# Channel attention on one core: VectorE's normalisation, its row statistics and the rounding of the next key in another order

## The chip, the cores and the metric

The kernel runs on one core of a Trainium2 chip. A core has TensorE (matmuls; PE in the profile), VectorE (DVE), ScalarE (ACT), GpSimd (POOL) and SyncE, which issues DMAs (SP). Each engine runs its own instructions in order, and semaphores join them. The metric is the device time of one execution in microseconds (us), as the median of several runs.

## The reference

Two layers of a gated cross-attention block on 16 x 64 rows of 512 elements. The change lies in the first of four sub-blocks, an attention over channels:

```
x = x + tanh(g_xattn[0]) * xattn0(layernorm(x), ctx)
x = x + tanh(g_ffn[0])   * clustered_linear(layernorm(x))
x = x + tanh(g_xattn[1]) * grouped_query_attention(layernorm(x), ctx, ctx, mask)
x = x + tanh(g_ffn[1])   * quantised_swiglu(layernorm(x))

def xattn0(x, init):                         # per batch: [64 channels, 512]
    q = einsum('dc,bct->btd', Wq, init) + bq
    k = einsum('dc,bct->bdt', Wk, init) + bk
    attention = softmax(einsum('btd,bds->bts', q, k), axis=-1)     # 512 x 512
    v = einsum('oc,bct->bto', Wv, x) + bv
    return einsum('bts,bsc->bct', attention, v)
```

Queries and keys are kept in two parts, a rounded one and its rest, so that a product in the short format keeps the precision of float32.

## The kernel before

`channel_attention` goes over eight tiles. A tile is 128 rows of x, that is two batches of 64 channels. Its scores are two times 512 x 512, cut into eight **units** of 128 x 512: units 0 to 3 belong to the first batch, 4 to 7 to the second. Every engine has its own function `tile(t, behind, ahead)` with a loop `for u in range(8)`, in which ifs on `u` put the other work of this tile, of the tile behind and of the tile ahead between the units' own steps. This order, written out by hand, is what each engine runs; nothing is sorted later.

One unit goes through the engines like this (lines of the profile):

- TensorE: `scores` (L423, L424), two matmuls into one of three banks `RR`. From unit 3 on they wait until the exponential three units back has freed the bank. The first unit of a batch (0 or 4) waits until VectorE has made `q_stk` and `k_lo` of that batch.
- VectorE: the negated row maximum `nmax` (L289), called "maximum u" below.
- ScalarE: the exponential with row sums (L192), `prob` and `zsum`.
- VectorE: `rz`, the reciprocal of the row sums (L267). GpSimd: `prob * rz` (L374), called "product u".
- TensorE: four transposes of `prob` (L431) into one of two banks `TP`, three units later. ScalarE (even units, L185) or VectorE (odd units, L271) copies the bank to `p_t`.

Between the units stand, for each tile:

- `project(t, n)` on TensorE (L400, L401): query (even n) and key (odd n) of batch n // 2, from `ctx_stk`. Those of the second batch of tile t stand in its unit 2, those of the first batch of tile t + 1 in unit 4.
- `qk_round` on ScalarE (L179): the rounded part, `q_stk` or `k_hi`, with its bias. `qk_rest` on VectorE (L255 for the query, L251 for the key): what the rounding left.
- `ctx_round` on ScalarE (L173) and `ctx_rest` on GpSimd (L357): the same for the context of the next tile, in unit 3.
- `normalize` on VectorE (L243): `xn` from x and the mean and deviation of its rows. TensorE's `values` (L409) reads it in unit 6.
- `outputs(t - 1)` on TensorE (L442): 16 matmul passes, in unit 3, right before the transposes of unit 0 and the scores of unit 4. `update(t - 1)` on VectorE (L277) adds them to x in unit 4, and `new_rows(t - 2)` (L283) takes the statistics of rows updated a tile before, for the next sub-block.

Constants that place the work: `OUTPUT = 3`, `PROJECT_A = 4`, `PROJECT_B = 2`, `UPDATE = 4`, `VALUE = 6`. Tiles 0, 1 and 7 are written out on VectorE, 2 to 6 are a hardware loop.

Of the kernel before, what the change touches and what calls it, by code (L numbers as in the profile page):

```python
# [66 lines left out]
def channel_attention(nc, d, c):  # L67
# [14 lines left out]
    with ExitStack() as ctx:  # L82
# [6 lines left out]
        def sem(name):  # L89
            return ctx.enter_context(nc.semaphore(name))  # L90
# [28 lines left out]
        s_sum, s_mv, s_var, s_rstd = sem("sums_ready"), sem("mean_var_ready"), sem("var_ready"), sem("rstd_ready")  # L119
# [11 lines left out]
        OUTPUT = 3  # L131


        PROJECT_A, PROJECT_B = 4, 2
# [26 lines left out]
        @block.scalar  # L161
        def _(act):
            act.dma_start(w_qk[:, :, :], d["WqkT"]).then_inc(s_wq, 16)
            act.dma_start(b_qk[:, :], d["b_qk"]).then_inc(s_wq, 16)
            act.dma_start(ident[:, :], d["ident"]).then_inc(s_par, 16)
            for b in range(2):
                act.dma_start(bv[:, b, :], d["bv"].partition_broadcast(P)).then_inc(s_par, 16)
            act.dma_start(tg[:, :], d["gates"].partition_broadcast(P)).then_inc(s_tg, 16)

            def ctx_round(t, b):  # L170

                act.wait_ge(s_ctx, 32 * t + 32)
                nc.scalar.activation(ctx_stk[:, b, :], ctx_two[:, b, :], ACT.Copy).then_inc(s_chi, 1)  # L173

            def qk_round(t, n):

                act.wait_ge(s_qk, 4 * t + n + 1)
                dst, is_k = (k_hi, 1) if n % 2 else (q_stk, 0)
                nc.scalar.activation(dst[:, n // 2, :], QK[n % 2][:, :], ACT.Identity,  # L179
                                     bias=b_qk[:, is_k:is_k + 1]).then_inc(qk_hi, 1)  # L180

            def evacuate(t, u):

                act.wait_ge(s_t, 8 * t + u + 1)
                nc.scalar.activation(p_t[:, u // 4, :, (u % 4) * P:(u % 4 + 1) * P],  # L185
                                     TP[0][:, :].rearrange("p (j t) -> p j t", j=KC),
                                     ACT.Copy).then_inc(pt_act, 1)

            def tile(t, behind, ahead):
                for u in range(8):  # L190
                    act.wait_ge(s_max, 8 * t + u + 1)
                    nc.scalar.activation(prob[:, u % 4, :], RR[u % 3][:, :], ACT.Exp,  # L192
                                         bias=nmax[:, u:u + 1], accum_out=zsum[:, u:u + 1])\
                      .then_inc(s_exp, 1)
                    if u == 1 and behind:
                        evacuate(t - 1, 6)
                    if u in (5, 7):
                        evacuate(t, u - 3)
                    if u == PROJECT_B + 1:
                        qk_round(t, 2)  # L200
                        qk_round(t, 3)
                    if u == OUTPUT and ahead:
                        ctx_round(t + 1, 0)
                        ctx_round(t + 1, 1)
                    if u == OUTPUT:
                        act.wait_ge(s_raw, 16)
                        nc.scalar.activation(ctx_hi[:, t, :], ctx_raw[:, t, :], ACT.Copy).then_inc(s_thi, 1)
                    if u == OUTPUT:
                        evacuate(t, 0)
                    if u == OUTPUT and not ahead:  # L210
                        act.wait_ge(s_w, 16)
                        nc.scalar.activation(w_hi[:, :, :], w_raw[:, :, :], ACT.Copy).then_inc(s_whi, 1)
                    if u == PROJECT_A and ahead:
                        qk_round(t + 1, 0)
                    if u == PROJECT_A + 1 and ahead:
                        qk_round(t + 1, 1)

            ctx_round(0, 0)
            act.wait_ge(s_wq, 32)
            nc.scalar.activation(w_qk_hi[:, :, :], w_qk[:, :, :], ACT.Copy).then_inc(s_wqk, 1)  # L220
            ctx_round(0, 1)
            qk_round(0, 0)
            qk_round(0, 1)
            act.dma_start(c["ctx_raw"][:, :, :], d["ctxT"].rearrange("(k p) n -> p k n", p=P)).then_inc(s_raw, 16)
            act.dma_start(w_raw[:, :, :], d["w_cl"].rearrange("(k p) n -> p k n", p=P)).then_inc(s_w, 16)
            act.dma_start(c["bias0"][:, :], d["bias0"].partition_broadcast(P)).then_inc(c["s_small"], 16)
            act.dma_start(c["assign_i"][:, :], d["assign"].partition_broadcast(CLUSTERS)).then_inc(c["s_small"], 16)
            act.dma_start(c["cluster_id"][:, :], d["cluster_ids"]).then_inc(c["s_small"], 16)
            act.wait_ge(s_tg, 16)
            nc.scalar.activation(tg[:, :], tg[:, :], ACT.Tanh).then_inc(s_tg, 1)  # L230
            tile(0, False, True)
            with act.Fori(1, TILES - 1) as t:
                tile(t, True, True)
            tile(TILES - 1, True, False)
            evacuate(TILES - 1, 6)

        @block.vector
        def _(dve):
# [3 lines left out]
            def normalize(t):  # L242
                nc.vector.tensor_scalar(xn[:, :], x_sb[:, t, :], mv[:, t, 0:1], rstd[:, t, :],  # L243
                                        ALU.subtract, ALU.mult).then_inc(s_xn, 1)
# [14 lines left out]
            def value(t):  # L259
                dve.wait_ge(s_v, t + 1)  # L260
                nc.vector.tensor_tensor(v_sb[:, :, :], OB[:, :].rearrange("p (j c) -> p j c", j=KC),
                                        bv[:, :, :].rearrange("p b c -> p (b c)").unsqueeze(1)
                                        .broadcast_to([P, KC, P]), ALU.add).then_inc(s_vsb, 1)

            def inverse(t, u):
                dve.wait_ge(s_exp, 8 * t + u + 1)
                nc.vector.reciprocal(rz[:, u:u + 1], zsum[:, u:u + 1]).then_inc(s_rz, 1)  # L267

            def evacuate(t, u):
                dve.wait_ge(s_t, 8 * t + u + 1)  # L270
                nc.vector.tensor_copy(p_t[:, u // 4, :, (u % 4) * P:(u % 4 + 1) * P],  # L271
                                      TP[1][:, :].rearrange("p (j t) -> p j t", j=KC))\
                  .then_inc(pt_dve, 1)

            def update(t):
                dve.wait_ge(s_o, t + 1)
                nc.vector.scalar_tensor_tensor(out=x_sb[:, t, :], in0=OB[:, :], scalar=tg[:, 0:1],  # L277
                                               in1=x_sb[:, t, :], op0=ALU.mult, op1=ALU.add)\
                  .then_inc(s_upd, 1)

            def new_rows(t):
                dve.wait_ge(s_upd, t + 1)
                nc.vector.bn_stats(c["bn6"][:, t, :], x_sb[:, t, :]).then_inc(s_sum, 1)  # L283

            def tile(t, behind, ahead):

                for u in range(8):
                    dve.wait_ge(s_r, 8 * t + u + 1)
                    nc.vector.tensor_reduce(nmax[:, u:u + 1], RR[u % 3][:, :], AX.X, ALU.max,  # L289
                                            negate=True).then_inc(s_max, 1)  # L290
                    if u == 0 and behind:
                        inverse(t - 1, 7)
                    if u and u != 4:
                        inverse(t, u - 1)
                    if u in (0, 2) and behind:
                        evacuate(t - 1, u + 5)
                    if u == PROJECT_B + 1:
                        qk_rest(t, 2)
                        qk_rest(t, 3)
                    if u == OUTPUT:  # L300
                        inverse(t, u)
                        if not behind:
                            dve.wait_ge(s_rstd, 1)
                        normalize(t)
                        if behind == 2:
                            new_rows(t - 2)
                    if u == UPDATE and behind:
                        update(t - 1)
                    if u in (4, 6):
                        evacuate(t, u - 3)  # L310
                    if u == PROJECT_A + 1 and ahead:
                        qk_rest(t + 1, 0)
                    if u == PROJECT_A + 2 and ahead:
                        qk_rest(t + 1, 1)
                    if u == VALUE + 1:
                        value(t)
# [16 lines left out]
            with dve.Fori(2, TILES - 1) as t:  # L333
                tile(t, 2, True)
# [1509 lines left out]
```

## Time and profile before

| | us |
|---|---|
| median of 3 runs | 847.76 |
| lowest and highest | 847.03, 848.78 |
| the profiled execution, its own time | 845.51 |
| its span, first to last instruction | 843.7 |
| channel attention within it | about 0 to 152 |
| VectorE busy over the whole span | 662.9 (79%) |
| TensorE busy over the whole span | 774.3 (92%) |

Channel attention takes the first 18% of the span. Times in the rows below are counted from the start of the span. A timeline row gives start, duration, engine, line, operation, tiles, shapes and, in square brackets, how long the engine sat idle before it and whose result ended that. Durations of one engine overlap a little: the next instruction starts before the last one's results are all written, so the cost of an instruction in a busy queue is the distance between starts, not the duration.

### The profile page before, as it was taken

What the parts mean: (1) busy time and instruction counts of PE and PEld (TensorE: products, weight loads), DVE (VectorE), ACT (ScalarE), POOL (GpSimd) and SP (SyncE); (2) the same over time, 40 slices, a digit from 0 to 9 for tenths busy, and PEclk for the clock granted to TensorE, in tenths of its full rate; (3) what the DMA queues carried; (4) which work ended last, traced back from release to release, by engine and by line L of the source; (5) the groups of instructions that cost most, each with busy time, mean ns of one, the idle gap of its engine ahead of it and who ended that gap; (6) DMA issues with size and microseconds to landing.
All of it is one profiled execution on the core that took longest, in us unless ns stands there. A gap on an engine that the chain in (4) does not pass through costs nothing.

```text
span 843.7 us, 12571 instructions
## 1 busy us (share of the span) xinstructions
PE 774.3 (92%) x4276; PEld 613.4 (73%) x4276; DVE 662.9 (79%) x1230; ACT 352.3 (42%) x1064; POOL 380.9 (45%) x324
## 2 busy tenths in 40 slices
PE   2898998888989999999999999999999999969975
PEld 1565565786867788888878888877888787757754
DVE  5788888888978877778788777787877778798972
ACT  2777776221334333333333333434333243237541
POOL 2787787415364433333253332434423333386541
PEclk9999999897999999999999999999999999989995
DMA  8310030101021111011020100102101020200101
GB/s 256 107 51 25 25 106 0 39 0 51 1 76 50 38 38 51 26 38 39 26 63 26 51 26 26 48 29 63 38 26 38 26 88 24 55 4 1 38 25 38
DMA packets 37460, 37.43 MB, mean 44 GB/s; under 512 B 2912, under 2 KB 27232, under 8 KB 37408
## 3 DMA queue, kind: packets, MB, share of 16 engines
q1 hardware_dynamic: 35184, 32.81, 13.3%
q10 hardware_dynamic: 2224, 3.94, 1.5%
q8 instruction: 31, 0.51, 0.3%
q14 instruction: 21, 0.17, 0.1%
HBM read 34.64 MB, written 2.10 MB: 44 GB/s over the span
## 4 chain that ended last, share of the span: by engine, by line
PE 63%; DVE 6%; POOL 4%; issue 3%; ACT 2%; POOLq 0%; DVEq 0%; ACTq 0%
PE QB L1478 6%; PE QB L1480 6%; PE SB L1598 6%; PE QB L1479 6%; PE ROW L1479 6%; PE ROW L1478 6%; PE ROW L1480 6%; PE KV L1478 4%; PE PB L1571 3%; PE KV L1479 3%; PE KV L1480 3%; DVE rope_b L1244 2%; PE KV L1662 2%; PE TB L1541 2%; POOL dense L976 1%
## 5 line engine op out<-in xcount | busy, mean ns | idle before, releaser
L976 POOL TENSOR_TENSOR dense<-rope_a,rope_b 128x512 f32<-128x512 f32 x62 | 79.4, 1280 | 167.5 <-DVE rope_b L1244 167.3
L1110 ACT ACTIVATE ot_hi<-PB 128x512 fp32r<-128x512 f32 x64 | 38.3, 599 | 198.4 <-PE PB L1571 198.2
L1101 ACT ACTIVATE e_sb<-masked,nmax 128x64 f32<-128x64 f32 x256 | 86.1, 337 | 58.1 <-DVE nmax L1273 57.7
L1478 PE MATMUL QB<-xT_hi,wq_lo 128*128 128x512 f32 x256 | 107.0, 418 | 0.0
L1479 PE MATMUL ROW<-wo_lo,ot_hi 128*128 128x512 f32 x256 | 101.7, 397 | 0.0
L1480 PE MATMUL QB<-xT_hi,wq_hi 128*128 128x512 f32 x256 | 101.7, 397 | 0.0
L1479 PE MATMUL QB<-xT_lo,wq_hi 128*128 128x512 f32 x256 | 101.5, 396 | 0.0
L1478 PE MATMUL ROW<-wo_hi,ot_lo 128*128 128x512 f32 x256 | 101.3, 396 | 0.0
L1480 PE MATMUL ROW<-wo_hi,ot_hi 128*128 128x512 f32 x256 | 101.0, 395 | 0.0
L1241 DVE TENSOR_TENSOR rope_a<-QB,rope 128x512 f32<-128x512 f32 x62 | 42.8, 691 | 72.7 <-PE QB L1480 72.5
L1282 DVE TENSOR_TENSOR p_sb<-e_sb,rz 128x256 f32<-128x256 f32 x64 | 86.8, 1356 | 2.2
L1244 DVE TENSOR_TENSOR rope_b<-QB,rope 64x512 f32<-64x512 f32 x124 | 85.4, 689 | 3.9
L374 POOL TENSOR_TENSOR prob<-prob,rz 128x512 f32<-128x512 f32 x64 | 66.3, 1045 | 22.7 <-DVE rz L267 21.6
L773 POOL TENSOR_TENSOR wq_lo<-raw,wq_hi 128x512 fp32r<-128x512 f32 x32 | 41.7, 1305 | 64.0 <-ACT wq_hi L765 64.0
L1598 PEld LDWEIGHTS SB<-k_rot,dense 128*128 128x128 f32 x512 | 64.3, 194 | 7.2 <-POOL dense L976 2.2
L1598 PE MATMUL SB<-k_rot,dense 128*128 128x64 f32 x512 | 67.0, 274 | 2.5 <-POOL dense L976 2.5
L192 ACT ACTIVATE prob<-RR,nmax 128x512 f32<-128x512 f32 x64 | 44.1, 690 | 34.6 <-DVE nmax L289 34.6
L1480 PEld LDWEIGHTS QB<-xT_hi,wq_hi 128*128 128x128 f32 x256 | 48.3, 189 | 11.7
L1480 PEld LDWEIGHTS ROW<-wo_hi,ot_hi 128*128 128x128 f32 x256 | 48.1, 188 | 11.7
L1478 PEld LDWEIGHTS ROW<-wo_hi,ot_lo 128*128 128x128 f32 x256 | 48.3, 188 | 11.5
L1479 PEld LDWEIGHTS ROW<-wo_lo,ot_hi 128*128 128x128 f32 x256 | 48.0, 188 | 11.0
L1479 PEld LDWEIGHTS QB<-xT_lo,wq_hi 128*128 128x128 f32 x256 | 48.7, 190 | 8.9
(200 smaller groups left out, 1902.2 us busy)
## 6 DMA issues: line engine op xcount, KB each, us to landing
raw<-in_wq SPq DMA_DIRECT2D x32, 256.0 KB, 2.7
raw<-in_wo SPq DMA_DIRECT2D x32, 256.0 KB, 2.6
ctx_two<-in_ctx SPq DMA_DIRECT2D x16, 256.0 KB, 3.8
x_sb<-in_x SPq DMA_DIRECT2D x8, 256.0 KB, 7.1
ctx_raw<-in_ctxT ACTq DMA_DIRECT2D x1, 2048.0 KB, 12.9
raw<-in_wv SPq DMA_DIRECT2D x8, 256.0 KB, 2.7
raw<-in_wk SPq DMA_DIRECT2D x8, 256.0 KB, 2.9
out<-x_sb SPq DMA_DIRECT2D x8, 256.0 KB, 2.0
```

The source lines that it names most:

```text
L192: nc.scalar.activation(prob[:, u % 4, :], RR[u % 3][:, :], ACT.Exp, bias=nmax[:, u:u + 1], accum_out=zsum[:, u:u + 1])\
L374: nc.gpsimd.tensor_tensor(prob[:, u % 4, :], prob[:, u % 4, :], rz[:, u:u + 1].broadcast_to([P, D]), ALU.mult).then_inc(s_p, 1)
L773: nc.gpsimd.tensor_tensor(lo, raw_piece(c, place, kind), hi, ALU.subtract).then_inc(c["s_piece"], 1)
L976: nc.gpsimd.tensor_tensor(dst, a, b, ALU.add).then_inc(s_rot, 1)
L1101: nc.scalar.activation(e_sb[:, r, :], masked[:, r, :], ACT.Exp, bias=nmax[:, r:r + 1], accum_out=zsum[:, r:r + 1]).then_inc(s_exp, 1)
L1241: nc.vector.tensor_tensor(a, v, cos.broadcast_to([P, 8, S]), ALU.mult).then_inc(s_parts, 1)
L1244: nc.vector.tensor_tensor(b[other], v[rows], sin[rows].broadcast_to([S, 8, S]), ALU.mult)\
L1282: nc.vector.tensor_tensor(p_sb[:, N % 2, :, :], e_sb[:, :, :], rz[:, :].unsqueeze(2).broadcast_to([P, 4, S]), ALU.mult).then_inc(s_p, 1)
L1478: nc.tensor.matmul(out, lhs[1], rhs[0], start=first, stop=False)
L1479: nc.tensor.matmul(out, lhs[0], rhs[1], start=False, stop=False)
L1480: return nc.tensor.matmul(out, lhs[0], rhs[0], start=False, stop=last)
L1598: mm = nc.tensor.matmul(SB_[:, S * a:S * a + S], q, keys[:, S * b:S * b + S], start=True, stop=True)
```

## The change

Three things are put elsewhere in the order of a tile; no instruction is added or removed, no size changes.

1. VectorE, unit 3: `normalize(t)` and the reciprocal of unit 3 stood behind `qk_rest(t, 2)` and `qk_rest(t, 3)`; now they stand ahead of them, and `normalize` also ahead of the reciprocal.
2. VectorE: `new_rows(t - 2)` stood at the end of unit 3; now it stands at the end of unit 2, ahead of maximum 3.
3. The first key of the next tile: ScalarE's `qk_round(t + 1, 1)` goes from unit 5 to unit 4, right behind the query's, and VectorE's `qk_rest(t + 1, 1)` from unit 6 to unit 5, again right behind the query's.

```diff
 (ScalarE, tile)
                     if u == PROJECT_A and ahead:
                         qk_round(t + 1, 0)
-                    if u == PROJECT_A + 1 and ahead:
                         qk_round(t + 1, 1)
 (VectorE, tile)
                     if u in (0, 2) and behind:
                         evacuate(t - 1, u + 5)
+                    if u == 2 and behind == 2:
+                        new_rows(t - 2)
+                    if u == OUTPUT:
+                        if not behind:
+                            dve.wait_ge(s_rstd, 1)
+                        normalize(t)
+                        inverse(t, u)
                     if u == PROJECT_B + 1:
                         qk_rest(t, 2)
                         qk_rest(t, 3)
-                    if u == OUTPUT:
-                        inverse(t, u)
-                        if not behind:
-                            dve.wait_ge(s_rstd, 1)
-                        normalize(t)
-                        if behind == 2:
-                            new_rows(t - 2)
 ...
                     if u == PROJECT_A + 1 and ahead:
                         qk_rest(t + 1, 0)
-                    if u == PROJECT_A + 2 and ahead:
                         qk_rest(t + 1, 1)
```

VectorE from the end of unit 2 to the start of unit 4, before, in the last tile (written out; the tiles of the loop have the same row of work): the first row is the copy that ends unit 2, the two maxima are 3 and 4.

```order
L271 COPY p_t<-TP 128x4x128
L289 TENSOR_REDUCE nmax<-RR 128x1
L267 RECIPROCAL rz<-zsum 128x1
L255 SCALAR_TENSOR_TENSOR q_stk<-QK,b_qk,q_stk 64x512
L251 SCALAR_TENSOR_TENSOR k_lo<-QK,b_qk,k_hi 128x512
L267 RECIPROCAL rz<-zsum 128x1
L243 TENSOR_SCALAR xn<-x_sb,mv,rstd 128x512
L283 BN_STATS bn<-x_sb 128x6
L289 TENSOR_REDUCE nmax<-RR 128x1
```

The same stretch now (line numbers are one or two lower):

```order
L270 COPY p_t<-TP 128x4x128
L282 BN_STATS bn<-x_sb 128x6
L288 TENSOR_REDUCE nmax<-RR 128x1
L266 RECIPROCAL rz<-zsum 128x1
L242 TENSOR_SCALAR xn<-x_sb,mv,rstd 128x512
L266 RECIPROCAL rz<-zsum 128x1
L254 SCALAR_TENSOR_TENSOR q_stk<-QK,b_qk,q_stk 64x512
L250 SCALAR_TENSOR_TENSOR k_lo<-QK,b_qk,k_hi 128x512
L288 TENSOR_REDUCE nmax<-RR 128x1
```

The statistics moved ahead of maximum 3, and the normalisation from behind the two rests to ahead of them, so that nothing stands between `k_lo` and maximum 4.

VectorE from maximum 5 to the copy of unit 6, before, in tile 0; the rests are those of tile 1's first batch:

```order
L289 TENSOR_REDUCE nmax<-RR 128x1
L267 RECIPROCAL rz<-zsum 128x1
L255 SCALAR_TENSOR_TENSOR q_stk<-QK,b_qk,q_stk 64x512
L289 TENSOR_REDUCE nmax<-RR 128x1
L267 RECIPROCAL rz<-zsum 128x1
L271 COPY p_t<-TP 128x4x128
L251 SCALAR_TENSOR_TENSOR k_lo<-QK,b_qk,k_hi 128x512
```

And now:

```order
L288 TENSOR_REDUCE nmax<-RR 128x1
L266 RECIPROCAL rz<-zsum 128x1
L254 SCALAR_TENSOR_TENSOR q_stk<-QK,b_qk,q_stk 64x512
L250 SCALAR_TENSOR_TENSOR k_lo<-QK,b_qk,k_hi 128x512
L288 TENSOR_REDUCE nmax<-RR 128x1
L266 RECIPROCAL rz<-zsum 128x1
L270 COPY p_t<-TP 128x4x128
```

The key's rest moved from behind maximum 6 and its copy to ahead of them. TensorE, GpSimd and SyncE run exactly the order they ran before.

## Rows read from the trace of the kernel before

**Rows 1.** Windows: stretch, length, busy us (x instructions) of each engine, PEclk, DMA.

```profile
core 0: us, PE busy (x) PEld busy (x) DVE busy (x) ACT busy (x) POOL busy (x), PEclk, DMA share, GB/s
69.12:85.21 16.09, 14.82 (x82) 9.29 (x84) 13.99 (x28) 11.89 (x27) 12.20 (x12) 1.00 0.12 33
155.00:160.00 5.00, 4.51 (x19) 4.51 (x20) 4.95 (x5) 2.50 (x5) 3.98 (x3) 0.50 0.18 53
300.00:500.00 200.00, 199.78 (x1119) 162.99 (x1118) 156.68 (x256) 72.77 (x262) 72.08 (x57) 1.00 0.13 36
```

**Rows 2.** Timeline of VectorE, maximum 0 to maximum 0 of tiles 3 and 4.

```profile
65.10 0.68 DVE L289 TENSOR_REDUCE nmax<-RR 128x1 f32<-128x512 f32 x1
...
69.12 0.69 DVE L289 TENSOR_REDUCE nmax<-RR 128x1 f32<-128x512 f32 x1 [0.48 <-PE RR L424]
...
71.24 0.76 DVE L255 SCALAR_TENSOR_TENSOR q_stk<-QK,b_qk,q_stk 64x512 fp32r<-64x512 f32 x1 [1.36 <-ACT q_stk L179]
72.03 0.75 DVE L251 SCALAR_TENSOR_TENSOR k_lo<-QK,b_qk,k_hi 128x512 fp32r<-128x512 f32 x1
...
72.76 1.18 DVE L243 TENSOR_SCALAR xn<-x_sb,mv,rstd 128x512 f32 x1
73.87 0.68 DVE L283 BATCH_NORM_STATS2 bn<-x_sb  x1
74.47 0.67 DVE L289 TENSOR_REDUCE nmax<-RR 128x1 f32<-128x512 f32 x1
...
76.32 0.67 DVE L289 TENSOR_REDUCE nmax<-RR 128x1 f32<-128x512 f32 x1
...
77.09 0.76 DVE L255 SCALAR_TENSOR_TENSOR q_stk<-QK,b_qk,q_stk 64x512 fp32r<-64x512 f32 x1
...
79.27 0.74 DVE L251 SCALAR_TENSOR_TENSOR k_lo<-QK,b_qk,k_hi 128x512 fp32r<-128x512 f32 x1
79.93 0.68 DVE L289 TENSOR_REDUCE nmax<-RR 128x1 f32<-128x512 f32 x1
...
81.19 0.68 DVE L289 TENSOR_REDUCE nmax<-RR 128x1 f32<-128x512 f32 x1
```

**Rows 3.** Timeline of TensorE: outputs, scores 4 and 5, scores 0 of the next tile.

```profile
69.01 3.65 PE L442 MATMUL OB<-p_t,v_sb 128*64 128x512 f32 x16
...
73.01 0.47 PE L423 MATMUL RR<-k_hi,q_stk 128*128 128x512 f32 x1
73.32 0.40 PE L424 MATMUL RR<-k_lo,q_stk 128*128 128x512 f32 x1
...
75.13 0.39 PE L424 MATMUL RR<-k_lo,q_stk 128*128 128x512 f32 x1
...
80.15 0.49 PE L423 MATMUL RR<-k_hi,q_stk 128*128 128x512 f32 x1 [0.91 <-DVE k_lo L251]
```

**Rows 4.** Timeline of GpSimd: products 7 and 2, then the context's rests.

```profile
65.94 1.04 POOL L374 TENSOR_TENSOR prob<-prob,rz 128x512 f32<-128x512 f32 x1 [0.22 <-DVE rz L267]
...
69.96 1.04 POOL L374 TENSOR_TENSOR prob<-prob,rz 128x512 f32<-128x512 f32 x1 [0.72 <-DVE rz L267]
72.38 2.72 POOL L357 TENSOR_TENSOR ctx_stk<-ctx_two,ctx_stk 64x512 fp32r<-64x512 f32 x2 [1.38 <-ACT ctx_stk L173]
```

**Rows 5.** Timeline of ScalarE: exponential 4 and the read of its sums.

```profile
75.17 0.69 ACT L192 ACTIVATE prob<-RR,nmax 128x512 f32<-128x512 f32 x1 [1.29 <-DVE nmax L289]
75.76 0.19 ACT L192 ACTIVATION_READ_ACCUMULATOR prob<-RR,nmax 128x1 f32 x1
```

**Rows 6.** Timeline of VectorE: maximum 5 of tile 0, maximum 0 of tiles 1 and 7.

```profile
28.65 0.69 DVE L289 TENSOR_REDUCE nmax<-RR 128x1 f32<-128x512 f32 x1 [0.28 <-PE RR L424]
...
33.53 0.68 DVE L289 TENSOR_REDUCE nmax<-RR 128x1 f32<-128x512 f32 x1
...
129.47 0.68 DVE L289 TENSOR_REDUCE nmax<-RR 128x1 f32<-128x512 f32 x1
```

**Rows 7.** Timelines of VectorE and GpSimd: normalisation and product 3 of tile 7.

```profile
137.12 0.53 DVE L243 TENSOR_SCALAR xn<-x_sb,mv,rstd 128x512 f32<-128x512 f32 x1
...
137.28 1.26 POOL L374 TENSOR_TENSOR prob<-prob,rz 128x512 f32<-128x512 f32 x1 [1.93 <-DVE rz L267]
```

## Prediction

> **What bounds the kernel now.** I looked first at where the change can act: only in channel attention, about 0 to 152 us. The windows [rows 1] show one tile of its loop, 16.09 us: VectorE is busy 13.99 us of it, TensorE 14.82 us, ScalarE and GpSimd about 12 us each. Two engines are nearly full and neither is quite, so the chain through both decides. The granted clock is 1.00 there (2.4 GHz).
>
> The timeline of VectorE [rows 2] gives the period from one maximum 0 to the next: 65.10 to 81.19, 16.09 us. I cut it at maximum 4 (74.47) into 9.37 and 6.72 us. In the first part VectorE is idle twice: 0.48 us ahead of maximum 3, for the scores, and 1.36 us ahead of the query's rest, for ScalarE's rounding. In the second it is never idle for long. TensorE [rows 3] waits 0.91 us ahead of scores 0 of the next tile, for the key's rest. So now the chain is: VectorE from maximum 0 on, through product 7 on GpSimd [rows 4] and the scores of unit 3 on TensorE back to maximum 3; then ScalarE's rounding, the two rests, the normalisation, the statistics, maximum 4; then VectorE's own queue to maximum 0.
>
> **Normalisation, unit 3.** Behind `k_lo` it costs 73.87 - 72.76 = 1.11 us between starts, all on the chain [rows 2]. Now it stands in the 1.36 us in which VectorE waits for ScalarE. It is 0.53 us long in tile 7 and 1.18 us in the loop [rows 7, 2], where it starts 0.38 us after GpSimd began the context's rests [rows 4]. In its new place it comes right behind a reciprocal whose product GpSimd is about to start. That is the situation of tile 7: the normalisation starts at 137.12 and takes 0.53 us, and the product, starting at 137.28, takes 1.26 instead of 1.04 us [rows 7, 4]. I take 0.53 us. Even 1.18 us would fit: from about 69.8 to 71.0, and the query's rest starts at 71.24. GpSimd loses some 0.2 us, but it has 1.38 us of idle time behind product 2 [rows 4]. Cost 0, gain 1.11 us of VectorE's chain. If the cover were gone it would cost 0.44 to 1.1 us.
>
> The 0.53 and the 1.18 us are to me one instruction with and without GpSimd on the shared way to memory. The Trainium skill (SBUF — State Buffer, Who interferes with whom) says that VectorE's two-port instructions and GpSimd's lock each other out, and that the one to issue first holds the ports for its whole length. By that rule the moved normalisation wins if it starts first, as in tile 7; if product 2 won, the normalisation would be held behind it, and that is rival A.
>
> **Statistics, unit 2.** They cost 74.47 - 73.87 = 0.60 us on the chain [rows 2]. Ahead of maximum 3 lies an idle time of 0.48 us, so they push it by at most 0.12 us, and by some 0.05 us if counted from where the copy lets the next instruction start. What hangs on maximum 3 is exponential 3, both roundings and both rests, and then scores 4. The key's rest ends at 72.03 + 0.75 = 72.78, and TensorE comes to scores 4 at 73.01 only, since the 16 output passes started at 69.01 [rows 3]. There are 0.23 us of room, so the push is covered. Bounds: 0, and 0.60 us if nothing covers it, of which 0.60 - 0.2 = 0.4 us would reach scores 4. I take 0, being nearest to the idle time in the row.
>
> **What is late next at maximum 4.** With 1.71 us gone from VectorE ahead of it, maximum 4 no longer waits for VectorE but for TensorE. The second matmul of scores 4 starts at 73.32 and lasts 0.40 us; with 0.04 us to the reader that is 73.76 instead of 74.47 [rows 3, 2]. The matmuls before it do not get earlier: they follow scores 3, which come from product 7, which starts at 65.94, right after maximum 0. So maximum 0 to maximum 4 becomes 73.76 - 65.10 = 8.66 us instead of 9.37. Only 0.71 of the 1.71 us are gained; the rest turns into a wait for TensorE.
>
> **The pair in unit 5.** The same instructions run between maximum 4 and the next maximum 0, in another order. Adding distances between starts [rows 2]: maximum 4 to 5, 1.85; on to the query's rest 0.77; on to the key's 0.79; on to maximum 6, 0.66; maximum 6 to 7 and 7 to 0 have the same three kinds of work each (a maximum, a reciprocal, a copy or sum), 1.26 each. Sum 6.59 us. The present order takes 6.72 us, the other bound. I take 6.6, since each of its distances was measured in that neighbourhood. Could anything be late inside it? Scores 5 are ready at 75.13 + 0.39 + 0.04 = 75.56 and maximum 5 now wants to start at 73.76 + 1.85 = 75.61: just in time. The key's rounding now runs ahead of exponential 5. Exponential 4 runs 0.70 us behind its maximum and takes 0.78 us with its sums [rows 5], the two roundings about 0.6 us each, so the key is rounded by about 76.4, well before VectorE wants it at 75.61 + 0.77 + 0.79 = 77.2. Maximum 6 comes at 77.8, exponential 6 ends 1.5 us later at 79.3, and scores 0 of the next tile can then start, instead of at 80.15 [rows 3], where they waited for the key's rest. They need about 0.8 us until they can be read, 80.1; maximum 0 comes at 73.76 + 6.6 = 80.4. So the wait of 0.91 us on TensorE goes, and VectorE's queue decides here.
>
> **The sum.** New period 8.66 + 6.6 = 15.26 us against 16.09. From maximum 0 of tile 1 (33.53) to that of tile 7 (129.47) lie six periods, 95.94 us [rows 6] (tile 1 has no statistics and is shorter). Now 6 x 15.26 = 91.56: a gain of 4.4 us. In tile 0, maximum 5 waits for TensorE and stays at 28.65; from there to 33.53 are 4.88 us, now 0.77 + 0.79 + 0.66 + 1.26 + 1.26 = 4.74: 0.1 us. Tile 7 rounds no next context and its maximum 4 follows TensorE's output passes almost at once already; nothing there but the shift. Together 4.5 us. Channel attention ends in a barrier of all engines, and the later parts run no changed instruction, so the gain should arrive at the end whole: the profiled execution would be 845.51 - 4.5 = 841.0. That execution lies 2.25 us under the median, so the median becomes 847.76 - 4.5 = 843.3 us.
>
> **Rivals.**
> A. *A smaller gain.* GpSimd gets the ports first: the normalisation ends at 69.96 + 1.04 + 0.53 = 71.53, the query's rest comes 0.3 us late, the key's ends near 73.1 to 73.2 and scores 4 slip by up to 0.2 us; six times that leaves 3.3 us. With 6.72 for the second part 0.7 us more go: 2.6 us, 845.2. For it: the 1.18 us in the loop. Against it: tile 7. Chance 0.18, taking 844.4 to 846.
> B. *No gain.* The waits move on: the statistics are uncovered (0.6 us late at maximum 3) and the normalisation is blocked as well. Then the query's rest starts 0.9 us late and scores 4 0.75 us late, and the period is 8.66 + 0.75 + 6.72 = 16.1, as now: 847.8. It needs both bad ends in every tile; the idle times in the rows speak against it. It is also what one would see if an order of semaphores I did not see held maximum 4. Chance 0.13.
> C. *Slower.* The parts behind start at another moment, and TensorE's clock there falls for longer. At 155 to 160 us, behind the idle time at the barrier, the granted clock is 0.50, that is 1.2 GHz, while TensorE is busy 4.51 of 5 us [rows 1]. At that level TensorE's work takes double the time, so each further us spent there costs half a us. The gain of 4.5 us is eaten when 9 us more run at 1.2 GHz, and at 13 us more the kernel is slower by 2 us: 849.8. Against it: from 300 to 500 us TensorE is busy 199.78 of 200 us at 1.00 [rows 1], and the idle time at the barrier does not change. Chance 0.07.
>
> **How the numbers follow.** The forecast has 0.62. About 0.2% (1.7 us) is what a measurement of this kernel can tell from no change. Forecast and A are faster, 0.80; B is the same, 0.13; C is slower, 0.07. The range: below, the forecast less another 1.4 us (medians of three runs spread over 1.75 us, and the second part might be a little shorter still), 841.9; above, A and the edge of B, where all bounds but one are bad (a gain of 1 us), 846.7. That leaves out most of B and C.
>
> **What the changed profile would show.** Right: maxima 0 of the loop 15.2 to 15.4 us apart; the normalisation at 0.53 us between maximum 3 and the query's rest, the product beside it 1.26 us; maximum 4 with an idle time of 0.7 to 1 us ahead of it, released by TensorE's scores; the wait of scores 0 for the key's rest gone; everything behind the barrier shifted by 4 to 5 us. Wrong: the normalisation at over 1.4 us, a query's rest more than 2.4 us behind maximum 3, scores 4 waiting for `k_lo`, or exponential 5 waiting for the key's projection. The whole would be wrong if the period fell and the end did not come earlier; then the clock windows behind 153 us are the place to look.

## The result and the profile after

| | before | after |
|---|---|---|
| median, us | 847.03 (7 runs) | 841.98 (7 runs) |
| lowest and highest, us | 845.32, 848.78 | 840.2, 843.5 |
| ratio, 95% interval | | 0.9941, 0.9927 to 0.9955 |
| the profiled execution, us | 845.51 | 842.73 |
| its span, us | 843.7 | 840.9 |

The change made the kernel 5.0 us faster; the interval of the ratio is 3.8 to 6.2 us. The forecast was a gain of 4.5 us and a time of 843.3 us, in a range from 841.9 to 846.7 us. The measured 841.98 us lie just above the lower end of that range. Of the 1.3 us below the forecast, 0.7 us come from the kernel before, whose median is 847.76 us over three runs and 847.03 over seven, and some 0.5 us from the gain.

The windows of the changed kernel, with one tile of the loop and a piece of tile 0 (columns as in [rows 1]):

```profile
core 0: us, PE busy (x) PEld busy (x) DVE busy (x) ACT busy (x) POOL busy (x), PEclk, DMA share, GB/s
67.11:82.38 15.27, 14.69 (x82) 9.33 (x80) 13.34 (x30) 11.88 (x28) 12.23 (x12) 1.00 0.11 34
...
28.00:31.00 3.00, 3.00 (x10) 2.41 (x9) 1.38 (x2) 1.99 (x5) 2.84 (x4) 0.50 0.00 0
```

A tile of the loop takes 15.27 us, 16.09 before. VectorE's busy time in it fell from 13.99 to 13.34 us although it runs the same instructions: that is the normalisation, 1.18 us before and 0.53 now. The second line, with a granted clock of 0.50, is a surprise and has a section of its own below.

VectorE, from maximum 0 of a tile to its maximum 7; it answers to [rows 2]:

```profile
67.11 0.68 DVE L288 TENSOR_REDUCE nmax<-RR 128x1 f32<-128x512 f32 x1
...
69.97 0.67 DVE L270 COPY p_t<-TP 128x512 f32<-128x512 f32 x1
70.56 0.68 DVE L282 BATCH_NORM_STATS2 bn<-x_sb  x1
71.16 0.67 DVE L288 TENSOR_REDUCE nmax<-RR 128x1 f32<-128x512 f32 x1
71.75 0.15 DVE L266 RECIPROCAL rz<-zsum 128x1 f32<-128x1 f32 x1
71.82 0.53 DVE L242 TENSOR_SCALAR xn<-x_sb,mv,rstd 128x512 f32 x1
72.68 0.16 DVE L266 RECIPROCAL rz<-zsum 128x1 f32<-128x1 f32 x1 [0.33 <-ACT prob L192]
73.26 0.76 DVE L254 SCALAR_TENSOR_TENSOR q_stk<-QK,b_qk,q_stk 64x512 fp32r<-64x512 f32 x1 [0.41 <-ACT q_stk L179]
74.05 0.75 DVE L250 SCALAR_TENSOR_TENSOR k_lo<-QK,b_qk,k_hi 128x512 fp32r<-128x512 f32 x1
75.76 0.69 DVE L288 TENSOR_REDUCE nmax<-RR 128x1 f32<-128x512 f32 x1 [0.96 <-PE RR L422]
...
77.62 0.68 DVE L288 TENSOR_REDUCE nmax<-RR 128x1 f32<-128x512 f32 x1
...
78.41 0.76 DVE L254 SCALAR_TENSOR_TENSOR q_stk<-QK,b_qk,q_stk 64x512 fp32r<-64x512 f32 x1
79.20 0.75 DVE L250 SCALAR_TENSOR_TENSOR k_lo<-QK,b_qk,k_hi 128x512 fp32r<-128x512 f32 x1
79.86 0.68 DVE L288 TENSOR_REDUCE nmax<-RR 128x1 f32<-128x512 f32 x1
...
81.12 0.68 DVE L288 TENSOR_REDUCE nmax<-RR 128x1 f32<-128x512 f32 x1
```

The single wait of 1.36 us ahead of the query's rest is now the normalisation and two waits of 0.33 and 0.41 us. The new wait is the 0.96 us ahead of maximum 4, and TensorE's scores (L422) end it. TensorE, output passes and scores 4, as in [rows 3]; the first row is scores 0 of the tile:

```profile
66.14 0.50 PE L421 MATMUL RR<-k_hi,q_stk 128*128 128x512 f32 x1 [0.32 <-ACT prob L192]
...
71.01 3.65 PE L440 MATMUL OB<-p_t,v_sb 128*64 128x512 f32 x16
...
75.01 0.47 PE L421 MATMUL RR<-k_hi,q_stk 128*128 128x512 f32 x1
75.32 0.40 PE L422 MATMUL RR<-k_lo,q_stk 128*128 128x512 f32 x1
```

Scores 4 run right behind the output passes and their transposes. The key's rest ended at 74.05 + 0.75 = 74.80, 0.21 us before they started. Scores 0 no longer wait for a key's rest (0.91 us before) but 0.32 us for exponential 6. GpSimd, product 2 and the context's rests, as in [rows 4]:

```profile
71.98 1.26 POOL L372 TENSOR_TENSOR prob<-prob,rz 128x512 f32<-128x512 f32 x1 [0.75 <-DVE rz L266]
74.40 2.53 POOL L355 TENSOR_TENSOR ctx_stk<-ctx_two,ctx_stk 64x512 fp32r<-64x512 f32 x2 [1.15 <-ACT ctx_stk L173]
```

Product 2 is 0.22 us longer, the context's rests are 0.19 us shorter than before (2.72). The normalisation used to start 0.38 us behind the start of the context's rests and now starts 0.16 us ahead of product 2: the collision moved from the one to the other.

### The profile page after: what moved, and what is told of

It is laid out like the page before. It is cut to its first block, busy times and chain, and to the rows that moved or that the text cites. A ratio compares the mean times of both kernels' runs of the same rounds, so it can differ in the third digit from the quotient of the medians.

```text
span 840.9 us, 12571 instructions
## 1 busy us (share of the span) xinstructions
PE 772.4 (92%) x4276; PEld 612.2 (73%) x4276; DVE 658.5 (78%) x1230; ACT 352.2 (42%) x1064; POOL 381.1 (45%) x324
## 4 chain that ended last, share of the span: by engine, by line
PE 61%; DVE 7%; POOL 4%; issue 3%; ACT 2%; POOLq 0%; DVEq 0%
PE SB L1596 6%; PE QB L1476 6%; PE QB L1478 6%; PE QB L1477 6%; PE ROW L1477 6%; PE ROW L1476 6%; PE ROW L1478 6%; PE KV L1476 4%; PE PB L1569 3%; PE KV L1478 3%; PE KV L1477 3%; DVE rope_b L1242 2%; PE KV L1660 2%; PE TB L1539 2%; POOL dense L974 1%
## 5 line engine op out<-in xcount | busy, mean ns | idle before, releaser
L771 POOL TENSOR_TENSOR wo_lo<-raw,wo_hi 128x512 fp32r<-128x512 f32 x32 | 41.2, 1297 | 30.7 <-ACT wo_hi L763 30.7
```

Of the source, the lines that this page charges most:

```text
L771: nc.gpsimd.tensor_tensor(lo, raw_piece(c, place, kind), hi, ALU.subtract).then_inc(c["s_piece"], 1)
```

## The experiments

All kernels stand beside the kernel before on the same chip. Two measures are given. The first is the ratio of the times, with its interval, turned into us of 847. The second comes from the profile of each: the period of the loop, its parts from maximum 0 to 4 and from 4 to the next 0, and six tiles, from maximum 0 of tile 1 to maximum 0 of tile 7, against 95.94 us [rows 6]. The last two columns, tile 0 (maximum 0 of tile 0 to that of tile 1) and the output passes of the last tile, are read in the section on the clock.

| kernel | time against before, us | period | 0 to 4 | 4 to 0 | six tiles | tile 0 | last passes |
|---|---|---|---|---|---|---|---|
| before | | 16.09 | 9.38 | 6.72 | 95.94 | 14.39 | 3.65 |
| before, second profile | +0.8 (-0.6 to +2.1) | 16.08 | 9.36 | 6.72 | -0.1 | 16.64 | 5.35 |
| after | -5.0 (-6.2 to -3.8) | 15.27 | 8.65 | 6.62 | -4.3 | 16.83 | 3.65 |
| after, second profile | -5.1 (-6.9 to -3.4) | 15.27 | 8.65 | 6.62 | -4.3 | 16.83 | 5.35 |
| norm_only | -2.4 (-3.6 to -1.3) | 15.40 | 8.65 | 6.74 | -3.6 | 17.43 | 3.65 |
| stats_only | -2.0 (-3.3 to -0.8) | 15.51 | 8.78 | 6.73 | -2.9 | 16.66 | 3.65 |
| pair_only | -0.8 (-2.2 to +0.4) | 15.96 | 9.37 | 6.59 | -0.8 | 16.61 | 3.65 |
| undo_stats | -4.7 (-6.1 to -3.2) | 15.27 | 8.65 | 6.62 | -4.3 | 16.55 | 3.65 |
| norm_unit2 | +0.3 (-0.6 to +1.4) | 16.08 | 9.46 | 6.62 | -0.1 | 16.79 | 5.35 |
| early_project | -2.9 (-4.1 to -1.7) | 15.70 | 9.08 | 6.62 | -1.7 | 16.27 | 3.65 |
| pe_filled | -5.9 (-7.3 to -4.7) | 15.27 | 8.66 | 6.62 | -4.3 | 14.11 | 3.65 |
| pe_filled_both | -5.3 (-7.0 to -3.4) | 15.28 | 8.66 | 6.62 | -4.3 | 13.38 | 3.65 |
| rests_mid | -5.4 (-6.9 to -3.8) | 15.27 | 8.65 | 6.61 | -4.3 | 14.43 | 3.65 |
| rests_filled | -6.1 (-7.5 to -4.7) | 15.27 | 8.65 | 6.62 | -4.3 | 14.20 | 3.65 |

**One part alone: normalisation.** My theory was that TensorE takes over at maximum 4 as soon as the normalisation is gone from behind the key's rest, with the statistics still there. The rival was that the parts add up.

```diff
                     if u == OUTPUT:
+                        if not behind:
+                            dve.wait_ge(s_rstd, 1)
+                        normalize(t)
                         inverse(t, u)
-                        if not behind:
-                            dve.wait_ge(s_rstd, 1)
-                        normalize(t)
-                        if behind == 2:
-                            new_rows(t - 2)
+                    if u == PROJECT_B + 1:
+                        qk_rest(t, 2)
+                        qk_rest(t, 3)
+                    if u == OUTPUT and behind == 2:
+                        new_rows(t - 2)
```

> Only the normalisation (with the reciprocal of unit 3) stands ahead of the two rests; statistics stay at the end of unit 3, behind the key's rest, and the next key is rounded and its rest made where they were. Theory (the cover decides, and TensorE takes over at maximum 4): the normalisation at 0.53 us; the key's rest ends near 72.8, the statistics take 0.60 us up to 73.3 (times of the tile shown for before), still ahead of 73.76, when TensorE has the scores; so maximum 4 waits about 0.4 us for scores and maximum 0 to maximum 4 is 8.66 us as in the changed kernel. Maximum 4 to maximum 0 stays 6.72 us. Period of the loop 15.38 to 15.40 us, change against before -3.7 to -4.3 us. Rival (the three parts add up, statistics give 0.60 us of their own): period 16.08 - 1.11 = 14.97 us at best or 15.87 us if only the 0.2 us that the statistics leave are gained.

VectorE in norm_only, from the key's rest to maximum 4:

```profile
74.06 0.75 DVE L251 SCALAR_TENSOR_TENSOR k_lo<-QK,b_qk,k_hi 128x512 fp32r<-128x512 f32 x1
74.73 0.68 DVE L283 BATCH_NORM_STATS2 bn<-x_sb  x1
75.79 0.69 DVE L289 TENSOR_REDUCE nmax<-RR 128x1 f32<-128x512 f32 x1 [0.38 <-PE RR L424]
```

The period is 15.40 us and 0 to 4 is 8.65, as expected; the statistics sit in the wait and 0.38 us of it are left. The time fell less than the six tiles did, 2.4 against 3.6 us, and misses the -3.7 that was expected at least. Its one profile has the longest tile 0 of all, 17.43 us; whether that is why stays open.

**One part alone: statistics.**

```diff
+                    if u == 2 and behind == 2:
+                        new_rows(t - 2)
...
-                        if behind == 2:
-                            new_rows(t - 2)
```

> Only the statistics are moved, from the end of unit 3 to the end of unit 2. Theory: maximum 3 comes up to 0.05 us later, the normalisation stays behind the key's rest at 1.18 us, and maximum 4 comes 0.55 us earlier than before, right behind the normalisation and with no wait for TensorE. Period of the loop 16.08 - 0.55 = 15.53 us, in the five tiles 2 to 6 only: change against before -2.7 us. Rival (statistics in unit 2 push maximum 3 by their 0.60 us and all behind it): period 16.1 us, no change.

VectorE in stats_only, the end of unit 3:

```profile
74.31 1.19 DVE L243 TENSOR_SCALAR xn<-x_sb,mv,rstd 128x512 f32 x1
75.42 0.68 DVE L289 TENSOR_REDUCE nmax<-RR 128x1 f32<-128x512 f32 x1
```

Maximum 4 follows the normalisation with no wait, the period is 15.51 us (15.53 expected), and maximum 0 to 3 is 4.05 us instead of 4.02: the push by the statistics is 0.03 to 0.04 us. Alone, this part gives 0.58 us a tile.

**One part alone: the key pair.**

```diff
                         qk_round(t + 1, 0)
-                    if u == PROJECT_A + 1 and ahead:
                         qk_round(t + 1, 1)
...
                         qk_rest(t + 1, 0)
-                    if u == PROJECT_A + 2 and ahead:
                         qk_rest(t + 1, 1)
```

> Only the next key is moved: rounded in unit 4, its rest made in unit 5. Theory: VectorE's queue from maximum 4 to maximum 0 goes from 6.72 to 6.60 us because maximum 6 and its reciprocal no longer stand behind the query's rest, nothing else moves, maximum 4 stays with VectorE. TensorE's wait of 0.91 us ahead of scores 0 goes down but gives nothing. Period 15.96 us, change against before -0.8 us. Rival (the wait of 0.91 us on TensorE was part of the chain): period 15.2 to 15.4 us, -4 us or more.

4 to 0 fell from 6.72 to 6.59 us and 0 to 4 stayed: period 15.96, as expected. TensorE in pair_only, scores 0:

```profile
81.22 0.50 PE L421 MATMUL RR<-k_hi,q_stk 128*128 128x512 f32 x1 [0.85 <-ACT prob L192]
```

TensorE's wait of 0.91 us for the key's rest went, and a wait of 0.85 us for exponential 6 took its place; VectorE's queue sets maximum 0 as before, so the wait for the key's rest was not part of the chain. The time alone could not tell this from no change.

**One part undone: statistics.** The changed kernel with `new_rows(t - 2)` back behind the key's rest.

> The changed kernel with the statistics put back to the end of unit 3, behind the key's rest (normalisation and key pair stay moved). Theory: the statistics fit into the 0.96 us that VectorE waits for scores 4 in the changed kernel, so the wait there shrinks to about 0.4 us and the period stays 15.27 us; change against before as the changed kernel, -4.5 to -5 us. Rival (the statistics' move gives a gain of its own): period 15.3 + 0.6 = 15.9 us, -1.5 to -2 us against before.

The wait ahead of maximum 4 shrinks from 0.96 to 0.38 us and the period stays 15.27 us. VectorE in undo_stats:

```profile
73.68 0.68 DVE L282 BATCH_NORM_STATS2 bn<-x_sb  x1
74.74 0.69 DVE L288 TENSOR_REDUCE nmax<-RR 128x1 f32<-128x512 f32 x1 [0.38 <-PE RR L422]
```

So in the changed kernel the move of the statistics is worth nothing. A move that gives 2.9 us in six tiles alone gives none beside the normalisation's, which gives 3.6 alone and leaves 0.4 us of room behind it: both remove work ahead of the same maximum, and TensorE caps the sum at 0.7 us a tile.

**The normalisation over a running product.** It is put ahead of the statistics in unit 2, where GpSimd is in product 1.

```diff
+                    if u == 2:
+                        if not behind:
+                            dve.wait_ge(s_rstd, 1)
+                        normalize(t)
                     if u == 2 and behind == 2:
                         new_rows(t - 2)
                     if u == OUTPUT:
-                        if not behind:
-                            dve.wait_ge(s_rstd, 1)
-                        normalize(t)
                         inverse(t, u)
```

> The changed kernel with the normalisation in unit 2, between the copy that ends the unit and the statistics, so that it starts about 70.6 us in the tile shown, while GpSimd is in the middle of product 1 (70.2 to 71.2). Theory (whichever of the two starts first keeps the other out): the normalisation is held until product 1 ends and takes about 1.1 us instead of 0.53; maximum 3 comes 1.1 us later, through the roundings scores 4 comes 0.9 us later, period of the loop 16.2 us, against before 0 to +1 us. Rival (no such lock, 0.53 us anywhere): maximum 3 comes 0.45 us later, scores 4 0.3 us later, period 15.55 us, against before -3 us.

VectorE in norm_unit2:

```profile
71.13 0.96 DVE L242 TENSOR_SCALAR xn<-x_sb,mv,rstd 128x512 f32 x1
72.01 0.68 DVE L282 BATCH_NORM_STATS2 bn<-x_sb  x1
```

GpSimd in the same kernel, products 0 and 1:

```profile
69.77 2.04 POOL L373 TENSOR_TENSOR prob<-prob,rz 128x512 f32<-128x512 f32 x2 [0.21 <-DVE rz L266]
```

The same instruction takes 0.96 us when it starts 0.68 us before the product's end, and 0.53 when it starts ahead of one. It is held, or slowed, by 0.43 us, a little less than until the product's end by its row. Placed here the normalisation costs 0.88 us between starts, and no wait of VectorE covers it; all of the change's gain is gone: period 16.08. Of these 0.88 us the rival gave 0.45 to the place alone. My 16.2 was 0.12 too high, for the most part because I had counted 1.1 us instead of 0.88.

**Projections earlier.** If TensorE's row of work from product 7 to scores 4 caps the gain, taking the projections of the second batch out of it should help.

```diff
-        PROJECT_A, PROJECT_B = 4, 2
+        PROJECT_A, PROJECT_B = 4, 1
...
                         normalize(t)
+                        qk_rest(t, 2)
+                        qk_rest(t, 3)
                         inverse(t, u)
-                    if u == PROJECT_B + 1:
-                        qk_rest(t, 2)
-                        qk_rest(t, 3)
```

> The changed kernel with the second batch's query and key projected in unit 1 instead of 2, rounded on ScalarE in unit 2, ahead of exponential 3; VectorE makes their rests in unit 3 as before, now between the normalisation and the reciprocal of unit 3. Theory (maximum 4 waits for TensorE's row of work from product 7 on: transposes, projections, scores 3, output passes, scores 4): without the projections in that row the output passes start as soon as VectorE's last copy of the tile behind is there, about 0.25 to 0.3 us earlier, maximum 0 to maximum 4 becomes 8.35 to 8.4 us, the period 14.95 to 15.0 us, and the time falls by 1.5 to 2 us below the changed kernel's. Rival (it is the key's rest that holds scores 4): it is ready earlier now as well, by 0.8 us, so the period would fall by up to 0.8 us, to 14.5 us. Third case (the output passes themselves or GpSimd hold): period unchanged at 15.27 us.

None of the three cases came: the period rose to 15.70 us. VectorE in early_project, maximum 0, maximum 2, the copy of the tile behind and maximum 4:

```profile
67.86 0.68 DVE L288 TENSOR_REDUCE nmax<-RR 128x1 f32<-128x512 f32 x1
...
70.75 0.69 DVE L288 TENSOR_REDUCE nmax<-RR 128x1 f32<-128x512 f32 x1 [0.89 <-PE RR L421]
...
71.43 0.67 DVE L270 COPY p_t<-TP 128x512 f32<-128x512 f32 x1
...
76.96 0.69 DVE L288 TENSOR_REDUCE nmax<-RR 128x1 f32<-128x512 f32 x1 [1.51 <-PE RR L421]
```

TensorE in the same kernel, scores 2 and the output passes:

```profile
70.33 0.39 PE L421 MATMUL RR<-k_lo,q_stk 128*128 128x512 f32 x1
...
72.21 3.65 PE L439 MATMUL OB<-p_t,v_sb 128*64 128x512 f32 x16 [0.59 <-issue]
```

The projections now stand ahead of scores 2, and maximum 2 waits 0.89 us. VectorE's copy of the tile behind starts 71.43 - 67.86 = 3.57 us after maximum 0 instead of 69.97 - 67.11 = 2.86 us. The output passes need that copy: they stand 0.59 us idle and start 0.11 us behind its end, 72.21 - 67.86 = 4.35 us after maximum 0 against 71.01 - 67.11 = 3.90 us in the changed kernel. That is about what the period lost, 0.43 us. I had counted what stood ahead of scores 3 and had not looked at what waits for scores 2.

## TensorE's clock in tile 0 and at the end

The span fell by 2.8 us only, while six tiles give 4.3. Maximum 0 of tile 1 is at 36.58 us, 3.05 us later than before: 0.61 us of that stand ahead of maximum 0 of tile 0 (19.75 against 19.14 us), 2.44 us in tile 0. For tile 0 the window 28 to 31 us above shows why: the granted clock is 0.50 there, 1.2 GHz. TensorE in the changed kernel, scores 4 of tile 0:

```profile
28.02 0.63 PE L422 MATMUL RR<-k_lo,q_stk 128*128 128x512 f32 x1
```

The same matmul before, where the window 24 to 28 us has 1.00:

```profile
26.39 0.39 PE L424 MATMUL RR<-k_lo,q_stk 128*128 128x512 f32 x1
```

So 3.05 us were lost up to tile 1 and 4.34 gained in six tiles: 1.3 us earlier at maximum 0 of tile 7. The last output passes of channel attention keep that distance. Before they are:

```profile
146.78 3.65 PE L442 MATMUL OB<-p_t,v_sb 128*64 128x512 f32 x16 [0.83 <-issue]
```

And in the changed kernel:

```profile
145.50 3.65 PE L440 MATMUL OB<-p_t,v_sb 128*64 128x512 f32 x16 [0.83 <-issue]
```

From their end to the end of the span are 693.3 us before and 691.8 after. These are the other 1.5 us of the 2.8, in a part of the kernel where no instruction was changed. In the fourteen profiles of the table this part takes 691.0 to 694.5 us; what moves it was not followed further.

At the start of the trace the matmuls tell the clock and the window does not. The window 20 to 24 us of the changed kernel reads 1.00, while its matmuls last 0.63 us:

```profile
20.00:24.00 4.00, 4.00 (x12) 3.03 (x11) 2.14 (x6) 2.31 (x6) 2.04 (x2) 1.00 1.03 398
```

```profile
20.69 0.63 PE L422 MATMUL RR<-k_lo,q_stk 128*128 128x512 f32 x1
```

Is it the change? The kernel before was profiled again, and so was the changed one.

> The kernel before, unchanged, for a second profile. Theory (whether TensorE's clock rises during the first scores is settled anew in every execution, whatever the kernel): the loop's periods are 16.08 us again, and tile 0 (maximum 0 to maximum 0) is either 14.4 us, as in the first profile, or 16.5 to 17.4 us, as in the changed kernel and four of the experiments; the span differs from 843.7 us by about the same 2 to 3 us in the second case. Rival (the long tile 0 belongs to the changed order): tile 0 is 14.4 us again.

> The changed kernel, unchanged, beside the two below on the same chip. Loop periods 15.27 us; against before -4.5 to -5.1 us; tile 0 at 14.3 or at 16.5 to 17.4 us.

The kernel before, second profile, windows in tile 0 and over the last output passes, and these passes:

```profile
core 0: us, PE busy (x) PEld busy (x) DVE busy (x) ACT busy (x) POOL busy (x), PEclk, DMA share, GB/s
...
28.00:30.00 2.00, 2.00 (x7) 1.67 (x8) 1.69 (x3) 1.00 (x3) 2.00 (x2) 0.50 0.00 0
...
149.80:155.10 5.30, 5.30 (x16) 1.70 (x16) 3.39 (x9) 0.00 (x0) 4.93 (x2) 0.68 0.01 3
```

```profile
149.77 5.35 PE L442 MATMUL OB<-p_t,v_sb 128*64 128x512 f32 x16 [0.83 <-issue]
```

Its tile 0 takes 16.64 us, its span 847.0, 3.3 us more than in the first profile of the same kernel. So the long tile 0 does not need the changed order; the first profile of before happened to be without it. The short one came with the changed order too, in rests_mid below, which fills nothing (14.43 us). Whether the change alters how often either comes is not shown. A second place of that kind are the last output passes: 5.35 us, with a granted clock of 0.68, instead of 3.65 in three of the fourteen profiles of the table, one of the kernel before and one of the changed kernel among them. Comparing before's second profile with the first of after, both with a long tile 0, maximum 0 of tile 1 stands at 36.58 us in both, and that of tile 7 at 132.45 and 128.18: 4.3 us from the six tiles, and the remaining 1.8 of 6.1 us in the span are the last passes (1.7 us) and what lies behind.

**Filling TensorE's idle time.** Transposes of a constant, whose results nobody reads: 18 in tile 0 ahead of scores 4, and in the second kernel 36 more ahead of the first scores.

```diff
+                    if u == OUTPUT and not behind:
+                        for _ in range(18):
+                            nc.tensor.transpose(OB[:, 0:P], w_v[:, :], ident[:, :])
```

> The changed kernel with 18 more transposes on TensorE in tile 0 only, behind the transposes of unit 0 and ahead of scores 4, into the bank OB that nobody reads before it is written anew. They add no result; they fill the idle time of about 3 us in which TensorE waits for the key's rest. Theory (the 3 us by which tile 0 was longer in the changed kernel's trace are TensorE's clock: matmuls of 0.63 us instead of 0.39 us up to 31 us): with TensorE busy there the clock is at 2.4 GHz from about 26 us on at the latest, maximum 0 of tile 0 to that of tile 1 falls from 16.8 us to 14.5 to 15 us, and the median is 1.5 to 2.5 us below the changed kernel's. Rival (the longer tile 0 comes from the moved work): tile 0 stays at 16.6 us or longer and the median is the changed kernel's or up to 1 us above.

> As the run before it, with 36 more such transposes ahead of tile 0, in the 8 us in which TensorE waits for the first key's rest. Theory (clock): the first scores run at 2.4 GHz too, maximum 0 to maximum 3 of tile 0 falls from about 4.1 to about 3.2 us, tile 0 takes 14.3 us or less and the median is 2 to 4 us below the changed kernel's. Rival (the clock does not depend on that idle time): as the changed kernel, or later where the transposes are still running when the key's rest is ready.

TensorE in pe_filled_both:

```profile
14.64 5.74 PE L471 MATMUL OB<-ident,w_v 128*128 128x128 f32 x36 [4.21 <-DMA w_v<-in_WvT]
...
20.46 0.39 PE L422 MATMUL RR<-k_lo,q_stk 128*128 128x512 f32 x1
```

With TensorE busy beforehand the first scores run at 0.39 us; in all other profiles they take 0.63. Maximum 0 to 3 of tile 0 falls to 2.33 us (3.0 to 4.2 elsewhere) and tile 0 to 13.38. That part of the theory is shown, by one profile against thirteen. But the filling work had to wait for the transfer of `w_v` until 14.64 and ran until 20.4 us, so maximum 0 came 1.2 us late, and the time gained nothing over the changed kernel. In the one profile of pe_filled the matmuls ran at 0.40 us from 20.9 us on, ahead of the filling at 22.6, so it shows nothing on the filling in tile 0; its times (839.5 to 843.4 us in 6 runs) overlap those of the changed kernel (840.2 to 844.6 in 13). The 1.5 to 2.5 us below the changed kernel that were expected of it are not shown.

**The first rests earlier.**

```diff
                 row_sums(nc, dve, c, t, s_sum, s_mv, t)
+                if t == 3:
+                    qk_rest(0, 0)
+                    qk_rest(0, 1)
...
-            qk_rest(0, 0)
-            qk_rest(0, 1)
```

> The changed kernel with the two rests of the first key and query of tile 0 made behind the statistics of x's tile 3 instead of behind all eight and the variance. VectorE has the same work up to the first maximum; only its wait of 1.48 us ahead of maximum 0, for the scores, should go. Theory: maximum 0 of tile 0 at about 17.7 us instead of 19.1 to 19.8, the rest as in the changed kernel, -1 to -1.5 us against it. Rival (TensorE stands idle again between the early scores and scores 3, and its clock stays at 1.2 GHz for longer): the gain at maximum 0 is given back by tile 0, which gets longer by 1 us or more, -0.5 to +0.5 us.

> Rests behind the statistics of x's tile 3, as in the run before, together with the 18 filling transposes in tile 0. Theory (both gains are independent: the one ahead of maximum 0, the other on TensorE's clock in tile 0): 1.2 + 1 to 1.5 us below the changed kernel, about 839.5 us where the kernel before takes 847. Rival (clock low from the early start on, so that the filling comes too early or too slow): as the better of the two alone.

Maximum 0 came at 18.89 us, not at 17.7. TensorE in rests_mid:

```profile
17.53 0.79 PE L422 MATMUL RR<-k_hi,q_stk 128*128 128x512 f32 x1 [7.21 <-DMA w_v<-in_WvT]
```

The rests were ready at 14.6 us, but TensorE's wait for `w_v`, written ahead of tile 0 though only unit 6 needs it, held the first scores until 17.5. Nor does 18.89 us stand out: in the profiles with the rests where they were, pe_filled_both left out, this maximum came at 18.28 to 20.19 us. rests_mid has a median of 840.60 us. rests_filled has the lowest median of all, 840.47 us, ratio 0.9928 (0.9912 to 0.9945), beside 841.28 us and 0.9940 (0.9919 to 0.9960) of the changed kernel on the same chip. The intervals overlap. Both beat the kernel before; whether either beats the changed kernel stays open, and the gain of 1 us and more that was expected of each did not show.

## Why the prediction was right

- *Maximum 4 will wait for TensorE, 8.66 us behind maximum 0.* Measured 8.65; the wait is 0.96 us. The chain product 7, scores 3, output passes, scores 4 was read from rows of before and did not move. norm_only and undo_stats show that it is a cap: with or without the statistics in front of it, 8.65.
- *Only 0.71 of the 1.71 us removed are gained.* Shown: normalisation alone 0.73 us in 0 to 4, statistics alone 0.60, both 0.73.
- *The normalisation takes 0.53 us in its new place and product 2 takes 1.26.* Both to the hundredth, with the normalisation starting 0.16 us ahead of the product as in tile 7. The rule of the Trainium skill (SBUF — State Buffer, Who interferes with whom) that the first to issue holds the ports was borne out in order: first ahead of product 2, it was not held; second behind product 1 (norm_unit2), it took 0.43 us longer. That the loser waits for the whole instruction of the winner is not quite what the rows show: held for the whole rest of the product it would have taken 0.68 + 0.53 = 1.21 us, and it took 0.96, 0.25 us less. Rows of GpSimd are rough.
- *The statistics push maximum 3 by 0 to 0.12 us, and the push is covered.* 0.03 to 0.04 us, covered by the 0.21 us of room at scores 4 (0.23 forecast).
- *4 to 0 takes 6.59 to 6.72 us, taken as 6.6.* 6.62, and pair_only 6.59. In tile 0, maximum 5 to the next maximum 0 takes 4.76 us instead of 4.89 (4.74 forecast).
- *The key's rounding ahead of exponential 5 holds nobody.* No wait for it appears; scores 0 wait 0.32 us for exponential 6 instead, which the prediction had named as the next to release them.
- *Six tiles give 4.4 us.* 4.3 us in the traces.
- *The rest of the time does not move.* This step was too simple, and 4.5 and 5.0 us part here or in the noise; the 0.5 us lie within the interval. The forecast took the clock to be a matter behind the barrier only (rival C) and took the profiled execution, 2.25 us under the median, as it came. Its sign for the changed profile, everything behind the barrier 4 to 5 us earlier, did not show in the first pair of profiles: the last passes end 1.3 us earlier, the span 2.8 us. Two profiles of the kernel before differ by 3.3 us in span, two of the changed kernel by 1.8 us. The first profile of the kernel before is 3.0 us shorter than its second up to maximum 0 of tile 7 and 1.7 us shorter in the last passes, and 1.4 us longer behind them. So single executions of one kernel differ by much of what the change gives, and one trace beside one other cannot size it. That it does not bias the medians is likely, since both kernels have the long and the short parts, but it is not shown; the forecast came near in spite of a premise that does not hold for a single execution.

Rivals A and B did not come in any part; norm_unit2 shows that the price which B put on a normalisation held by a product was real. Held so, in a place where nothing covers it, it puts maximum 4 at 9.46 instead of 8.65 us after maximum 0, and the whole gain goes.

## What to carry to other kernels

Before adding up what several moves remove ahead of one wait, look for the second chain that ends at the same wait and how far behind it is: here it was 0.7 us behind, so the first move that removed that much took all there was, and the others gave nothing there. Before moving work into an idle time, look at what the neighbouring engine runs then: here the same normalisation took 0.53 us ahead of GpSimd's product and 0.96 us when it started behind one. And where a gain is a few us, compare periods within the loop, and profile the old kernel twice: here two profiles of it differed by 3.3 us.

## What the runs showed of the hardware that I had not expected

- The first scores run at 0.63 us a matmul instead of 0.39 in every profile but the one in which TensorE was kept busy beforehand. In five of the fourteen profiles the matmuls were down to 0.40 us or less by 21.4 us and stayed there, and tile 0 took 13.4 to 14.4 us. In the other nine the matmuls behind TensorE's idle time in tile 0 took 0.63 us until between 29 and 35 us, and tile 0 took 16.3 to 17.4 us. An idle time of 3.3 us stands in profiles of both kinds; behind it the granted clock read 0.50 in the second profile of the kernel before and 1.00 in the first.
- The last 16 output passes, behind a stretch in which TensorE had waited several times for single products and copies, took 3.65 or 5.35 us in profiles of the same kernel, with a granted clock of 1.00 or 0.68. What decides it stays open.
- The normalisation of the loop's tiles has three lengths, by what GpSimd does: 0.53, 0.96 and 1.18 us.
